# Second attention of a fused block: where the maximum products stand among the shifted products and the value block

## The reference

```python
q = (hidden_state @ Wq + bq).reshape(b, l, KVH, GROUPS, HD).transpose(0, 2, 3, 1, 4)
k = (encoder_hidden_state @ Wk + bk).reshape(b, s, KVH, HD).transpose(0, 2, 1, 3)
v = (encoder_hidden_state @ Wv + bv).reshape(b, s, KVH, HD).transpose(0, 2, 1, 3)
...
scores = jnp.einsum('bkgld,bksd->bkgls', q, k) * scale
scores = scores + encoder_attention_mask[:, :, None, :, :]
attn = jax.nn.softmax(scores, axis=-1)
out = jnp.einsum('bkgls,bksd->bkgld', attn, v)
```

## Time and profile before

| | us |
|---|---|
| median of 3 executions | 6087.48 (6083.95 to 6108.49) |
| the profiled execution, its time | 6107.38 |
| its span | 6105.6 |
| second attention, first unit to last value block | 2920.1 to 4180 |
| of it with shifted products and units side by side | 2959.9 to 4111 |
| PE busy, whole span | 5393.1 (88%) |
| VectorE busy, whole span | 3562.3 (58%) |
| ScalarE busy, whole span | 2786.4 (46%) |

### The profile page before, as it was taken

How to read it: one execution, slowest core, us unless ns; L and a number is a source line. 1 busy time by engine, 2 the same in 40 slices (tenths; PEclk the granted TensorE clock), 3 DMA queues, 4 the chain that set the end, 5 groups by cost and what they waited for, 6 DMA issues and landing times. The chain is left out here.

```text
span 6105.6 us, 69068 instructions
## 1 busy us (share of the span) xinstructions
PE 5393.1 (88%) x26050; PEld 1873.7 (31%) x26050; DVE 3562.3 (58%) x4608; ACT 2786.4 (46%) x5261; POOL 1471.4 (24%) x708
## 2 busy tenths in 40 slices
PE   6988999999797999987688888886879999997999
PEld 2333333433232333323122222221322333322444
DVE  4548677877343777741788888871228777761010
ACT  2423333333231566651477777773214666663111
POOL 0004333333000566650000000000004666662000
PEclk8988999999898899998799999996988999998999
DMA  3233333332212333213111111112233332302000
GB/s 105 94 106 107 86 87 93 96 91 77 89 55 55 64 74 66 62 34 111 34 28 28 28 28 28 29 22 78 76 79 63 65 73 53 70 26 97 21 21 14
DMA packets 459769, 383.48 MB, mean 63 GB/s; under 512 B 169809, under 2 KB 359094, under 8 KB 458764
## 3 DMA queue, kind: packets, MB, share of 16 engines
q1 hardware_dynamic: 459428, 379.00, 23.3%
HBM read 242.83 MB, written 135.14 MB: 62 GB/s over the span
## 5 line engine op out<-in xcount | busy, mean ns | idle before, releaser
L2174 DVE TENSOR_REDUCE att_part<-att_scores 128x1 f32<-128x423 f32 (+1 forms) x2304 | 1190.6, 579 | 425.3 <-PE att_scores L2021 423.8
L2138 ACT ACTIVATE att_prob<-att_scores 128x512 f32<-128x512 f32 (+1 forms) x1920 | 993.8, 600 | 549.0 <-PE att_scores L2033 548.7
L2476 DVE TENSOR_REDUCE att_part<-att_scores 128x2 f32<-128x802 f32 x1024 | 964.7, 989 | 218.9 <-PE att_scores L2383 216.0
L2157 POOL TENSOR_TENSOR att_acc<-att_acc,att_prob 128x1024 f32<-128x1024 f32 (+1 forms) x416 | 985.1, 2368 | 441.1 <-ACT att_prob L2138 439.1
L2462 ACT ACTIVATE att_prob<-att_scores 128x512 f32<-128x512 f32 (+1 forms) x1664 | 884.6, 599 | 317.7 <-PE att_scores L2397 313.1
L2021 PE MATMUL att_scores<-att_k,att_q 97*128 97x423 f16 (+1 forms) x2304 | 816.7, 358 | 83.9 <-DMA att_q<-in_c_q 59.8
L2033 PE MATMUL att_scores<-att_q,att_k 98*128 98x512 f16 (+1 forms) x1920 | 721.7, 383 | 13.6 <-ACT att_prob L2138 13.4
L2157 POOL TENSOR_TENSOR att_acc<-att_prob 128x1024 f32<-128x1024 f32 x32 | 75.6, 2363 | 2521.2 <-ACT att_prob L2138 2521.2
L1264 POOL TENSOR_TENSOR scan_z<-scan_r,scan_states 128x512 f32<-128x512 f32 x256 | 410.4, 1603 | 1107.5 <-DVE scan_states L1297 1091.3
L2397 PE MATMUL att_scores<-att_q,att_k 49*128 49x512 f16 (+1 forms) x1664 | 562.2, 400 | 36.6 <-ACT att_prob L2462 36.3
L2383 PE MATMUL att_scores<-att_k,att_q 48*128 48x401 f16 x2048 | 393.7, 351 | 184.4 <-DVE att_part L2476 160.9
(11 more groups left out here) (294 smaller groups left out, 6108.6 us busy)
## 6 DMA issues: line engine op xcount, KB each, us to landing
v<-scan_val SPq DMA_DIRECT2D x96, 256.0 KB, 2.3
att_v<-v SPq DMA_DIRECT2D x32, 768.0 KB
att_spread<-recips SPq DMA_DIRECT2D x64, 256.0 KB
mix_plane<-in_mask SPq DMA_DIRECT2D x16, 800.5 KB, 6.7
att_k<-k1hi SPq DMA_DIRECT2D x32, 400.2 KB
att_k<-k3hi SPq DMA_DIRECT2D x32, 400.2 KB
scan_x<-in_ctx_t SPq DMA_DIRECT2D x12, 1024.0 KB, 9.3
o<-att_out SPq DMA_DIRECT2D x32, 256.0 KB, 2.0
```

The lines of the kernel that those rows point to most:

```text
L2138: nc.scalar.activation(prob[g % NP][0:kw(kt), h, :], scores2[0:kw(kt), n % RING2, :], ACT.Exp).then_inc(exped, 1)
L2157: nc.gpsimd.tensor_tensor(acc[s % 2][0:kw(kt)], so_far[0:kw(kt), 0:PH, :], prob[g % NP][0:kw(kt), 0:PH, :], ALU.add).then_inc(padded, 1)
L2174: nc.vector.reduce_max(part[q % 2][:, hc, piece:piece + 1], scores1[:, bank["piece", p], 0:PIECE], AX.X).then_inc(reduced, 1)
L2476: nc.vector.reduce_max(part[q % 2][:, :, ec, piece], scores1[:, bank["unit", p], :, 0:PIECE], AX.X).then_inc(reduced, 1)
```

## The change

The number of units due is now counted by slots: each tile has five, one behind each of the four shifted products and one behind the value block. Per 13 tiles, 32 units go to 65 slots. ScalarE's place of the copy of the maxima follows the same count.

```diff
--- before.py
+++ after.py
@@ -2228,9 +2228,11 @@
     LOADS = 2 * SIDES * len(HALF)
     VLOADS = 2
 
-    def units_by(g):
-
-        return min(N * UNITS, AHEAD + (g + 1) * UNITS // NT)
+    SLOTS = QUAD + 1
+
+    def units_by(g, slot=SLOTS - 1):
+
+        return min(N * UNITS, AHEAD + (g * SLOTS + slot + 1) * UNITS // (NT * SLOTS))
 
     def turn_after(q):
 
@@ -2422,11 +2424,14 @@
                             pe.wait_ge(topsent[s % 2], 16 * SIDES * (s // 2 + 1))
                         for h in range(QUAD):
                             shift(s, kt, h)
-                            if issued < units_by(g):
+                            while issued < units_by(g, h):
                                 next(one)
                                 issued += 1
                     if g >= LAG:
                         mix(*divmod(g - LAG, NT))
+                    while g < G and issued < units_by(g):
+                        next(one)
+                        issued += 1
                 for _ in one:
                     pass
 
@@ -2460,7 +2465,7 @@
                         n = g * QUAD + h
                         act.wait_ge(shifted, n + 1)
                         nc.scalar.activation(prob[g % NP][0:kw(kt), h, :], scores2[0:kw(kt), n % RING2, :], ACT.Exp).then_inc(exped, 1)
-                        while rounds < N and turn_after(rounds) <= min(units_by(g), units_by(g - 1) + (h if h < QUAD - 1 else UNITS)):
+                        while rounds < N and turn_after(rounds) <= units_by(g, h if h < QUAD - 1 else SLOTS - 1):
                             round_top(rounds)
                             rounds += 1
                 drain(N - 1)
```

## The result

The change takes the kernel from 6086.05 us (median of 5 executions, 6079.93 to 6108.49) to 6028.71 us (5 executions, 6015.62 to 6037.24): a ratio of 0.990, 95% interval 0.9883 to 0.9916, or 57 us less. The forecast was 54 less, 6033.5.

What follows compares the result with a forecast made beforehand. No engine is full; loops of latencies through too short rings bound it. Sequences of 35.25 instead of 36.7 us save 43 over about 30, the clock 11: 54 less, 6033.5 us from the median, range 5990 to 6095.

Steps and rivals of the forecast that it cites:

- The two-unit tile's: Loop in tiles with two units: first exponential, fourth shifted product, value block, next tile's first shifted product, its exponential; 2.45 us.
- the burst's: Loop in three-unit tiles: third unit waits for the first reduction's place in a ring of two; 3.15 us, costing 0.70.
- The third unit leaves the burst: Three-unit tiles: no unit among the shifted products waits for its own tile's reduction, so the 3.15 us loop is gone.
- the loop carries a unit in every tile: Loop through the first exponential: a unit adds 0.18 us, so both kinds of tile take 2.63 us; bounds 2.45 to 2.79.
- not nothing (2.45): Rival: the unit costs nothing in the loop, tiles take 2.45 us, a sequence 32.9, the kernel 5963; chance 0.06.
- Do the reductions keep up: Two tiles followed on VectorE: every unit finds its place free, the one ahead of the value block only by 0.1 us.
- the rival of waits that only move: Unit ahead of the value block waits for late reductions, eating the gain; 6070 to 6095 us, middle 6080, chance 0.14.
- that of units for reductions falls below 100: Sign that the forecast is right: the units' total wait for reductions, 250 us before, falls below 100.
- The turn, the copy, the multiplication: Charges per sequence: turn in tile 9 0.8 us, copy of the sums in tile 2 0.15, VectorE multiplication in tile 11 0.1.
- The clock: PE's drops to 1.2 GHz, some 18 in the stage costing 22 us, follow PE's pauses; half go, 11 us back.
- The clock stays up: Rival: PE's clock stays up throughout, 22 us come back instead of 11; 6022 us, chance 0.18.
- The clock drops more often: Rival: PE's runs broken by short waits hold the clock down; 6130 us at three drops a sequence, chance 0.07.

## Why the prediction was right

*What bounds the kernel.* Both loops stood as read. The two-unit tile's was confirmed where a unit put into it lengthened it by 0.16 to 0.17, the burst's where a reduction shorter by 0.42 shortened the tile by 0.42, and with 41% less work on VectorE the change's ordinary tiles kept their 2.61 to 2.63.

*The third unit leaves the burst; the loop carries a unit in every tile.* The forecast was 2.63 us for both kinds of tile; measured 2.63 and 2.61. The unit cost 0.16 to 0.18 as taken from the same instruction elsewhere, not nothing (2.45) and not its whole record (2.79). The rule of the Trainium skill on weight loads (TensorE: Matmul & The Clock Gate, "The mechanism"), as the prediction read it, would have added 0.09 a tile. It did not: S0 starts 0.19 behind the unit, with its load inside that. The same section also lets a load go ahead into a background weight buffer, and that agrees with these rows.

*Do the reductions keep up.* The unit ahead of the block was to have 0.1 us of margin. It starts 0.13 behind S3, just as its place comes free, and the block 0.49 behind S3. In the kernel with only the two-unit tiles moved that unit starts together with S3 and the block again 0.49 behind it, so the 0.13 costs nothing. The kernel with only the third unit moved shows what the rival of waits that only move would have looked like: with the second unit behind S1, two shifted products earlier, it waits 0.71. One sign missed: "that of units for reductions falls below 100" was read from the row of the weight loads, which shows 189; in PE's own row the wait is 8.5.

*The turn, the copy, the multiplication.* 0.8, 0.15 and 0.1 were charged; tile 9 takes 3.43 (0.82 more than its kind), tile 2 2.77 (0.14 more) and tile 12, behind the multiplication, 2.66 (0.03 more). The last and the rounding of 2.61 to 2.63 make the sequence 35.06 instead of 35.25, and the sum of these terms 50 us where 43 were forecast.

*The clock.* This step was wrong in its reason, and that its size came out near was luck. "I take the drops to follow PE's pauses" does not hold: the kernel with only the two-unit tiles moved keeps the burst's pauses and has 2 drops and none, and before has all its drops in one of its six tiles with that pause. "I take half the drops away" came true in number (16 to 6 and 8), but one drop in each profile of the change is long, so that the time at 1.2 GHz in the first 30 sequences fell only from 61 us to 37 and 44. In numbers, the mean sequence lay 0.8 us above the undisturbed one before, and lies 0.5 to 0.6 above it now, so 6 to 9 us came back where 11 were forecast. 50 and about 8 make the 57 of the medians.

*The rivals.* "The clock stays up" did not come, although a sibling with four slots shows that it could. "The clock drops more often" did not come: the rule of the Trainium skill on clock swings with cycling PSUM places (TensorE: Matmul & The Clock Gate, "A second HAM failure mode: psum-queue depth-cycling") is not borne out as a rule against spreading: with the units spread over four slots the clock was 1.00, and before, with its bursts, had the most drops.

## What to carry to other kernels

When no engine is full, write down the loop that sets a period as a chain of rows, with each step's duration, and cost a move by whether the instruction lies in that chain: here some 0.17 us in a loop taken in every tile bought the end of a 0.70 wait in six tiles of thirteen. Two halves of a reordering need not add up, because one makes the slack that the other uses; try them apart before keeping one. And compare undisturbed periods and mean pace separately, since an order can win in latency and lose the win in clock.

## What was not expected of the hardware

PE's clock went down or stayed up with the order of the same instructions, at nearly the same load: from 1.00 (four slots, PE's records covering 89% of the steady part) through 0.98 (the change, 88%) to 0.97 (before, 85%), but 0.99 and 1.00 also with only the two-unit tiles moved, at 83%. So how busy PE is over such a stretch does not decide it. Where in the work a drop began was fixed, tile 2 of a sequence in nearly every case, while whether it came differed from sequence to sequence: in before the drops lie one, two or four sequences apart. In each of the change's two profiles one drop also lasted much longer than elsewhere: one sequence took 42.70 us at 0.76, that is 20 us at 1.2 GHz. And the last sequence, without units, took 33 or about 50 us by the clock that the execution happened to have there; both were seen with the kernel before, with the change and with only the two-unit tiles moved.
